# A fused Mamba and gated FFN layer in fp32: Silu of z read from PSUM, softplus as one function, dt products in row pairs, conv in place, the first norm on ScalarE, and new order lists

## The reference

```python
xz = jnp.einsum('bld,ed->ble', x, W_in)            # 256 -> 1024
xi, z = jnp.split(xz, 2, axis=-1)                  # 512 each
xc = sum((xpad[:, k:k + L, :] * conv_w[:, k] for k in range(4)))
u = silu(xc + conv_b)
dbl = jnp.einsum('blc,ec->ble', u, W_xproj)        # 512 -> 16 + 16 + 16
dt = jax.nn.softplus(jnp.einsum('blr,cr->blc', dbl[..., :16], W_dt) + b_dt)
# scan over the tokens, 16 states for each of the 512 channels:
h = h * exp(dt * A) + (dt * u) * B ;  y = sum over states of h * C
y = (y + u * D_skip) * silu(z)
x = layernorm(x + y @ W_out.T)
x = layernorm(x + (silu(x @ wg.T) * (x @ wu.T)) @ wd.T)   # 256 -> 768 -> 256
```

## Time and profile before

| | |
|---|---|
| median of 3 runs | 1802.77 us |
| span of the profiled execution | 1797.7 us (5.1 us below the median of the runs, which have what lies around it too) |
| PE busy | 1734.7 us, 96% |
| ACT busy | 1712.9 us, 95% |
| DVE busy | 1675.1 us, 93% |
| POOL busy | 1477.8 us, 82% |
| ACT table loads | 125 of 1283 ns |

### The profile page before, as it was taken

One profiled execution on the slowest core, in us unless ns is written; L12 is line 12 of the kernel. 1 busy time (PEld: TensorE's weight loads), 2 busy tenths in 40 slices (PEclk: granted clock), 3 DMA queues, 4 the chain that ended last, 5 costly groups with the idle time before them and its releaser, 6 DMA issues.

```text
span 1797.7 us, 40378 instructions
## 1 busy us (share of the span) xinstructions
PE 1734.7 (96%) x15678; PEld 1214.6 (68%) x15678; DVE 1675.1 (93%) x1970; ACT 1712.9 (95%) x2907; POOL 1477.8 (82%) x852
## 2 busy tenths in 40 slices
PE   7779999999999999999999999999999999999997
PEld 3456676767667676676767667676676767667676
DVE  5999999999999999999999999999999999999974
ACT  6999999999999999999999999999999999999971
POOL 5897987979889797997979889797987979889850
PEclk9999999999999999999999999999999999999999
DMA  7040211304013030211304013040311304022000
GB/s 211 1 121 1 56 65 15 118 11 121 3 16 118 15 118 2 66 68 16 118 10 123 2 15 119 14 119 1 74 60 16 118 13 121 1 39 83 1 25 24
DMA packets 171487, 100.57 MB, mean 56 GB/s; under 512 B 139408, under 2 KB 157584, under 8 KB 163232
## 3 DMA queue, kind: packets, MB, share of 16 engines
q1 hardware_dynamic: 171296, 97.98, 19.3%
HBM read 88.52 MB, written 9.44 MB: 54 GB/s over the span
## 4 chain that ended last, share of the span: by engine, by line
PE 48%; ACT 26%; DVE 11%; issue 9%; POOL 5%; SPq 0%; DMA 0%; ACTq 0%; POOLq 0%; DVEq 0%
PE ring L1162 17%; PE tp L1141 13%; ACT decay L706 8%; ACT hT L713 7%; PE yb L1155 7%; DVE h L917 6%; POOL drive L568 4%; PE ring L1254 3%; PE ring L1230 3%; DVE acc L938 3%; PE ring L1199 2%; ACT L743 1%; ACT acc L722 1%; PE ring L1220 1%; ACT dt L760 1%
## 5 line engine op out<-in xcount | busy, mean ns | idle before, releaser
L568 POOL TENSOR_TENSOR drive<-dtu,b_all 128x1024 f32<-128x1024 f32 x511 | 1204.4, 2389 | 17.6 <-DVE acc L938 9.2
L706 ACT ACTIVATE decay<-dt,a_neg 128x512 f32<-128x512 f32 x1024 | 705.0, 717 | 7.2 <-DVE h L917 6.4
L917 DVE TENSOR_TENSOR_SCAN h<-decay,h,drive 128x512 f32<-128x512 f32 x512 | 620.5, 1267 | 9.4 <-ACT decay L706 6.4
L1141 PEld LDWEIGHTS tp<-ident,h 128*128 128x128 f32 x4096 | 463.9, 141 | 240.1 <-issue 124.1
L917 DVE TENSOR_TENSOR_SCAN h<-decay,drive 128x512 f32<-128x512 f32 x512 | 592.3, 1208 | 29.2 <-ACT decay L706 25.3
L713 ACT ACTIVATE hT<-tp 128x512 f32<-128x512 f32 x1024 | 595.9, 618 | 11.8 <-PE tp L1141 10.9
L1141 PE MATMUL tp<-ident,h 128*128 128x128 f32 x4096 | 564.1, 277 | 37.9 <-ACT hT L713 29.1
L1155 PE MATMUL yb<-hT,diag_c 128*32 128x128 f32 x8192 | 275.8, 277 | 6.5 <-ACT yt L734 5.3
L1155 PEld LDWEIGHTS yb<-hT,diag_c 128*32 128x32 f32 x8192 | 210.7, 110 | 82.5 <-issue 48.8
L1162 PE MATMUL ring<-xt,w_in 128*128 128x512 f32 x512 | 245.2, 602 | 2.3 <-ACT acc L754 2.3
L1162 PE MATMUL ring<-xt,w_g 128*128 128x512 f32 x360 | 170.6, 596 | 0.0
(11 more groups left out here) (132 smaller groups left out, 1648.1 us busy)
## 6 DMA issues: line engine op xcount, KB each, us to landing
b_all<-bc_scratch SPq DMA_DIRECT2D x63, 1024.0 KB, 7.2
xt<-in_xT SPq DMA_DIRECT2D x16, 512.0 KB, 4.7
res<-in_x SPq DMA_DIRECT2D x16, 512.0 KB, 6.6
out<-res SPq DMA_DIRECT2D x15, 512.0 KB, 2.9
c_col<-bc_scratch SPq DMA_DIRECT2D x256, 2.0 KB, 2.4
bc_scratch<-dbl SPq DMA_DIRECT2D x16, 64.0 KB, 1.6
b_all<-bc_scratch SPq DMA_DIRECT2D x2, 512.0 KB, 4.4
w_g<-in_w_gT SPq DMA_DIRECT2D x1, 768.0 KB, 6.3
```

Source lines behind the costliest of these rows:

```text
L568: tt(drive[:, j % 4, :, :], src, b_all[:, n:n + 2, :], ALU.mult).then_inc(g_dr, 1)
L706: act(decay[decay_slot(k.parity, i)][:, :], dt[:, cb, :], ACT.Exp, scale=a_neg[:, cb, n:n + 1]).then_inc(a_da, 1)
L917: nc.vector.tensor_tensor_scan(h[:, h_slot(k.parity, q), at:at + T, i % 4], decay[decay_slot(k.parity, i)][:, :], drive[:, (i // 2) % 4, i ...
L1141: last = nc.tensor.transpose(tp[g % 2][:, b * P:(b + 1) * P], h[:, h_slot(k.parity, q), t0:t0 + TS, :].rearrange("p t s -> p (t s)"), iden ...
```

## The change

- `silu_z` reads z's PSUM bank itself; `copy_z` goes. The bank is free only when the Silu is done.
- Softplus is one activation function, read from the dt bank. The bias b_dt comes in as one more row of the product: `w_dt` has the row, and `dbl` has a 1 there (`one_at`, added while it is copied).
- `dbl` holds the two halves of the tokens on the partition halves 0 to 63 and 64 to 127, in 256 columns. `dt_pair` makes two blocks at a time with four products of 64 rows and 256 columns; the upper and the lower half of the rows go to different banks. `dt` now has two buffers, by parity of the chunk.
- The conv runs in place in `u`; `acc` goes.
- The first norm is applied by ACT; `normalise` has a parameter for it.
- `hT` has nine slots for eight. `out` and `down` are cut into halves that can be placed apart.
- The tables are new, and the first and last chunk use the steady ones (only POOL's first stays). The three output products that stood in the last chunk's table now stand in PE_END. SP stores `dbl` with two DMAs, and loads W_dt and b_dt twice.

```diff
-HTS = 8
+HTS = 9
-    (2, 2): [("hT", 4), ("xi", 0), ("z", 2), ("hT", 5)], (2, 3): [("hT", 6)], (3, 0): [("hT", 7)],
+    (6, 0): [("sz", 0), ("y", 0), ("sz", 1), ("norm", 0), ("u", 0), ("sz", 2), ("sz", 3), ("hT", 17), ("hT", 18), ("x1T", 0), ("x1T", 1), ("u", 1), ("hT", 19), ("hT", 20), ("u", 2), ("u", 3), ("tanh", 0)],
...
+PE_FIRST = PE_LAST = PE_SIDE
+ACT_FIRST = ACT_LAST = ACT_SIDE
+DVE_FIRST = DVE_LAST = DVE_SIDE
+POOL_LAST = POOL_SIDE
...
-                wait(eng, v_dt, k.count(2, -1 + cb // 2))
+                wait(eng, v_y, k.count(4, cb - 7))
...
-                act(acc[:, cb, :], bank(k, "xi", cb)[:, :], ACT.Identity, scale=cw[:, cb, KW - 1:KW],
+                act(u[:, k.parity, cb, :], bank(k, "xi", cb)[:, :], ACT.Identity, scale=cw[:, cb, KW - 1:KW],
...
             def silu_z(k, cb):
-                eng.wait_ge(a_z, k.count(4, cb + 1))
-                act(sz[:, cb, :], sz[:, cb, :], ACT.Silu).then_inc(a_sz, 1)
+                wait(eng, p_z, k.count(4, cb + 1))
+                wait(eng, g_y, k.count(4, cb - 3))
+                act(sz[:, cb, :], bank(k, "z", cb)[:, :], ACT.Silu).then_inc(a_sz, 1)
...
+                act(dbl[:, :], bank(k, "xproj", 0)[:, 0:T // 2], ACT.Identity, bias=one_at[:, 0:1]).then_inc(a_dbl, 1)
+
+            def softplus(k, p):
+                wait(eng, p_dt, k.count(4, 2 * p + 2))
+                wait(eng, g_dtu, k.count(2, p - 3))
                 for b in range(2):
+                    act(dt[:, k.parity, 2 * p:2 * p + 2, b * T // 2:(b + 1) * T // 2],
+                        bank(k, "dt", 2 * p + b)[:, :].rearrange("p (c t) -> p c t", c=2), ACT.Softplus).then_inc(a_dt, 1)
...
-            def softplus_max(k, half):
-                stt(dt[:, two, :], dt[:, two, :], 40.0, acc[:, two, :], ALU.min, ALU.max).then_inc(v_dt, 1)
...
+            def dt_pair(k, p):
+                wait(eng, a_dbl, k.count(1, 1))
+                for c in range(2):
+                    for b in range(2):
+                        rows = slice(b * RB, (b + 1) * RB)
+                        block = slice((2 * p + c) * P, (2 * p + c + 1) * P)
+                        last = mm(bank(k, "dt", 2 * p + b)[:, c * T // 2:(c + 1) * T // 2], w_dt[rows, block], dbl[rows, :],
+                                  start=True, stop=True)
+                        if c == 1:
+                            last.then_inc(p_dt, 1)
```

More of the change, by code:

```diff
@@ L31 @@
 KW = 4
+RB = 64
 HD = 768
@@ L51 @@
 PE_SIDE = {
[L52 to L62, removed]
+    (0, 1): [("xi", 0)], (0, 3): [("sum", 14), ("sum", 15)], (1, 0): [("turn", 3)], (1, 1): [("xi", 1)],
@@ L63 @@
+    (10, 2): [("up", 3)], (11, 0): [("dt", 1), ("sum", 8), ("sum", 9)],
+    (11, 2): [("turn", 1), ("gate", 4), ("gate", 5)], (12, 0): [("up", 4)], (12, 1): [("up", 5)],
+    (12, 3): [("sum", 10), ("sum", 11)], (13, 1): [("down", 0, 0), ("turn", 2)], (13, 3): [("down", 0, 1)],
+    (14, 1): [("sum", 12)], (14, 3): [("down", 1, 0), ("down", 1, 1)], (15, 3): [("sum", 13)],
 }
 ACT_SIDE = {
[18 rows of a table removed]
[16 rows of a table added]
 }
 DVE_SIDE = {
-    (2, 1): [("skip", 3)], (3, 3): [("conv", 0, 0), ("r1", 0)], (4, 2): [("r1", 1)],
-    (5, 3): [("max", 1), ("norm", 0), ("conv", 0, 1), ("conv", 1, 0), ("conv", 1, 1), ("conv", 2, 0), ("conv", 2, 1), ("conv", 3, 0), ("conv", 3, 1)],
@@ L106 @@
-ACT_FIRST = {
[16 rows of a table removed]
[L123 to L129, removed]
+    (2, 1): [("diag", 1), ("gate", 3)], (5, 0): [("diag", 2)], (5, 1): [("diag", 3)], (6, 0): [("std", 0)],
+    (6, 1): [("heads", 0)], (7, 0): [("dtu", 1)], (12, 0): [("dtu", 0)], (12, 1): [("std", 1)],
@@ L267, in in_chunk @@
 def in_chunk(item, kind):
-    what, i = item
+    what, i, *part = item
     if what in TAIL or item == ("turn", CB - 1):
@@ L272, in in_chunk, with banks_of @@
     return what not in HEAD or kind != "last"
+def banks_of(item):
+    what, i, *part = item
+    if what == "dt":
+        return [(what, 2 * i), (what, 2 * i + 1)]
+    if what == "sum" or what.startswith("end_") or part and part[0] > 0:
+        return []
+    return [(what, i)]
 def owner(what, i, c):
@@ L288, in products_in_order @@
 def products_in_order(chunks):
-    before = [item for at in sorted(PE_FIRST) for item in PE_FIRST[at] if item[0] in HEAD]
-    order = [(what, i, 0) for what, i in before]
+    order = [(what, i, 0) for item in PROLOGUE for what, i in banks_of(item)]
     for c in range(chunks):
@@ L294, in products_in_order @@
         table = table_of(kind, PE_SIDE, PE_FIRST, PE_LAST)
-        order += [(what, i, owner(what, i, c)) for at in sorted(table) for what, i, *_ in table[at]
-                  if what != "sum" and not what.startswith("end_") and in_chunk((what, i), kind)]
+        order += [(what, i, owner(what, i, c)) for at in sorted(table) for item in table[at]
+                  if in_chunk(item, kind) for what, i in banks_of(item)]
     return order
@@ L622, in item @@
                     scale_and_shift(k + (-2 if i else -1), i)
-                if what == "std" and i == 0 and not head:
-                    eng.wait_ge(v_x1, (k + -1).count(4, 4))
                 if what == "first_diag":
@@ L630, in item @@
                     diagonals(k, i)
-                if what == "yield" and head:
-                    wait(eng, v_conv, conv_steps(k + 1, 1))
                 if what == "heads" and head:
@@ L810, in item @@
                         copy_y(k + -1, i)
-                if what == "norm" and late:
-                    normalise(k + -2)
+                if what == "norm" and i == 1 and late:
+                    normalise(k + -2, 1)
+                if what == "norm" and i == 0 and tail:
+                    normalise(k + -1, 0)
                 if what == "x1T" and tail:
@@ L1025, in _ @@
             for cb in range(CB - 1):
-                conv(k0, cb, 0)
-                conv(k0, cb, 1)
+                for step in range(KW - 1):
+                    conv(k0, cb, step)
             eng.wait_ge(l_w, ALL_LOADED)
@@ L1246, in gate_up, with down, dense @@
                                    for d in range(DH)], done)
-            def down(k, i):
-                if i == 0:
+            def down(k, i, half):
+                if i == 0 and half == 0:
                     wait(eng, v_hid, k.count(6, 6))
-                for half in range(2):
-                    tb = 2 * i + half
-                    for m in range(HB):
-                        last = mm(bank(k, "down", i)[:, half * DM:(half + 1) * DM],
-                                  hidden_block(m)[:, tb * P:(tb + 1) * P],
-                                  w_d[:, m, :], start=m == 0, stop=m == HB - 1)
-                last.then_inc(p_down, 1)
-            def dense(k, what, i):
+                tb = 2 * i + half
+                for m in range(HB):
+                    last = mm(bank(k, "down", i)[:, half * DM:(half + 1) * DM], hidden_block(m)[:, tb * P:(tb + 1) * P],
+                              w_d[:, m, :], start=m == 0, stop=m == HB - 1)
+                if half == 1:
+                    last.then_inc(p_down, 1)
+            def dense(k, what, i, *part):
                 if what == "xi":
@@ L1290, in item @@
                 elif in_chunk((what, *of), kind):
-                    c = owner(what, *of, k.index)
-                    room(place[what, *of, c])
+                    c = owner(what, of[0], k.index)
+                    for name, i in banks_of((what, *of)):
+                        room(place[name, i, c])
                     dense(k + (c - k.index), what, *of)
@@ L1397, in _ @@
             eng.wait_ge(l_in[0], 16)
-            for at, (what, i, c) in enumerate(order):
-                if c > 0 or what not in HEAD:
-                    break
+            for what, i in PROLOGUE:
                 if (what, i) == ("xi", 1):
@@ L1410, in _ @@
                     eng.wait_ge(l_w, ALL_LOADED)
-                room(at)
+                for name, n in banks_of((what, i)):
+                    room(place[name, n, 0])
                 if what == "xproj":
```

256 lines of the change are left out of this document (89 added, 167 removed), and 63 rows, old and new, of tables (ACT_FIRST, ACT_LAST, ACT_SIDE).

## The result

The changed kernel takes 2083.67 us (median of 4 runs, 2083.41 to 2088.32), the kernel before 1802.77 beside it. The ratio is 1.157, with an interval of 1.1549 to 1.159. Now and then an execution of a kernel falls into a much slower state (one of the four before took 2961.67 us); medians and ratios here leave such executions out. The forecast was 1755 us with a range to 1788: wrong in sign, and by 329 us.

The account below looks back on a forecast made before the run. PE and ACT were both taken as full. Savings of 40.6 us (14 steady chunks), 5 (chunk 0) and 2 (last chunk), with 0.5 added (head), gave span 1750.6, plus 5.1 about 1755; own range 1742 to 1768, 8-in-10 range 1734 to 1788.

Parts of the forecast that it names:

- the one on SP: SP's store of dbl becomes two; it need only finish before the next chunk's drives, with 15 us POOL idle: 0.
- row pairs: PE's dt products: eight of 64 rows and 256 columns share the array, 1.72 us saved a chunk; shape changes add 0.25.
- Rival 2: PE's dt row pairs do not share the array: +1.72 us on 15 chunks, 1781 us; chance 0.12.
- PE's idle time: PE in steady chunks: half of its idle 1.05 us goes, since ACT is no longer full.
- the 104.9 of the forecast: Steady chunk: 107.8 us less 2.4 of PE work and half of PE's idle 1.05, so 2.9 saved.
- rival 3: PE waits on its two product banks (z on Silu, gate on DVE): 1.6 us a chunk, 1777 us; chance 0.18.
- the block without a decay: ACT between the switches to and from the Silu table: about 13 us without decays, DVE's cover lacking about 1.
- Rival 4: Slower: ACT's 13 us block and DVE's conv steps don't overlap, DVE lacks decays: 4.8 us a chunk, 1822; chance 0.08.
- the drain: ACT table loads: the skill page's 1.38 us per load, 8.3 us for six, left out because the trace disagrees.
- Chunk 0: First chunk: between POOL's 94.9 us busy and the 104.1 it took; 99 taken, 5 saved.
- Tail: The 54.8 us behind the last chunk's last scan: same work, change 0.
- The output products: PE, last chunk: those moved behind the last scan cost there what they save here; the chunk saves 2 us.

Follow-up runs that it names:

- run 1: Changed kernel with SP's store of out moved behind all other DMA issues of the chunk; 1798.76 us, ratio 0.9994 to the kernel before.
- run 5: As run 1, with heads in POOL's list of chunk 0 moved from (8, 0) to (6, 1); 1793.42 us, ratio 0.9963 to the kernel before.
- run 3: Kernel before, with only ACT's second norm moved from (6, 3) to (14, 3); 2089.07 us, ratio 1.1605.
- run 6: As run 1, with ACT's second norm moved from (14, 3) to (13, 3); 1819.12 us, ratio 1.0103 to the kernel before.
- run 12: As run 5, with the first norm back on DVE ahead of the conv steps; 1797.88 us, ratio 0.9984 to the kernel before.
- Runs 7 and 10: Last chunk's lists changed, down and output products earlier: 7 on run 1, 1804.07 us; 10 on run 5, smaller, PE's list alone, 1795.03 us.
- run 8: Kernel before, with SP's store of out moved behind all other issues of the chunk; 1800.16 us, ratio 0.9999.
- run 9: As run 5, with turn 3 behind xi 1, tanh 1 and 2 behind evacuations 23 and 25, evacuations 55 and 56 earlier; 1891.85 us, ratio 1.051.
- run 11: As run 5, with the four products of a dt pair issued by row half, not in turn; 1793.85 us, ratio 0.9968 to the kernel before.

## Why the prediction was wrong

From its span of 1750.6 to the measured 2081.6 it is 331 us. Run 1 takes back 281.3 of that (2081.6 - 1800.3), run 5 another 8.7 (to 1791.6), and 41 remain.

**The step that failed** is the one on SP: "SP only has to be done before the next chunk's drives, which have 15 us of POOL idle behind them: 0". It counted the added DMA and not what stands ahead of it. The second norm's move from (6, 3) to (14, 3) has no term in the sum at all; with its work on ACT unchanged, it was put at nothing without a reason. But the store of `out` waits for it, at the head of a queue that everything for the next chunk has to pass. The row was there to be read: in the kernel before SP already waited 66 us a chunk for that norm.

```profile
SPq L488 <- ACT res L772: 132.1, 2, 66.4
```

The norm now came 49 us later, with 23 DMAs behind the store that the next chunk needs, and the chunk grew by 20.6 to 21.3 us; run 3 shows that this move alone does it (1.1605), run 1 that the queue carries it. No rival had this mechanism; the slower one was put on ACT's block against the conv steps.

**PE, row pairs: right.** The pair shares the array, 0.86 us and 0.20 for changes of shape. Rival 2 is refuted. In run 5 PE's busy time is 105.1 on average against 106.8, 1.7 saved and not 2.4; where the other 0.7 went was not traced.

**PE's idle time: wrong in sign.** Half of 1.05 was to go, "since ACT is no longer full". It grew to 1.5 (105.35 - 104.25 = 1.1 and 107.85 - 105.96 = 1.9). Together with the 0.7 above, this 1.0 is the 1.7 us by which a steady chunk of run 5 misses the 104.9 of the forecast. In run 5 PE waits for evacuations 2.5 us in two chunks where it was 1.3, though ACT idles 5 to 6 us a chunk:

```profile
PE tp L1030 <- ACT hT L648: 2.5, 7, 0.9
```

I read this as PE waiting for the place of an evacuation in ACT's list, and not for ACT's load: moving ACT's norm (run 6) or taking one off it (run 12, with more for DVE) freed nothing. No run shows it by itself. This is rival 3 in kind, though on the transpose banks, and small: 106.5 a chunk and not 104.9, 21 us over 13 chunks.

**ACT: right.** Six table loads a chunk and softplus as in the first rows below (two steady chunks of run 1), the block without a decay 12.75 us in run 5 (13 forecast), behind which DVE waited 0.9 (1 forecast). Rival 4 didn't come: DVE waited 2.6 us for decays in two chunks. On the drain that the Trainium skill (page "ScalarE: Activation LUTs", section "What ACT_TABLE_LOAD costs") adds to a load: there is none in these rows either. The last two rows are from run 5, and the decay starts as the load of 1.28 us ends.

```profile
L641 ACT ACT_TABLE_LOAD x6 | 7.7, 1283 | 0.1
...
L688 ACT ACT_TABLE_LOAD x4 | 5.1, 1283 | 0.1
...
L688 ACT ACTIVATE dt<-ring 128x512 f32<-128x512 f32 x8 | 4.4, 597 | 0.0
L673 ACT ACT_TABLE_LOAD x2 | 2.6, 1283 | 0.0
```

```profile
928.14 1.28 ACT L641 ACT_TABLE_LOAD   x1
929.43 1.91 ACT L641 ACTIVATE decay<-dt,a_neg 128x512 f32<-128x512 f32 x3
```

**Chunks 0 and 1.** Chunk 0 was forecast at 99 and is 103.5 even in run 5. PE idles 26 us in it, but it idled 28 in the kernel before too, so this does not say why the 5 us did not come; only the place of heads was tested. Chunk 1 takes 111.0 and not 104.9. It starts on a PE at half the clock: 50 matmul records in its first 5.6 us, 77 in those of chunk 3. Yet the clock is not the main cause: in the changed kernel chunk 1 had a granted clock of 1.00 and took 110.3, as the row below shows. What holds it was not traced.

```profile
139.67:250.01 110.34, 107.12 (x1004) 76.56 (x1006) 101.89 (x117) 100.44 (x175) 96.13 (x51) 1.00 0.18 50
```

**Tail: wrong.** "Same work, 0" was measured as +6.6 (61.4 against 54.8). The output products that "cost there what they save here" saved next to nothing in the last chunk, 101.2 against 101.7: PE's work there fell by 5.5 us (99.6 to 94.1) and its idle time grew by nearly as much. Runs 7 and 10 suggest that they are in the tail's sum, but not how to get them out.

The 41 us are then: 13 steady chunks 21, chunk 1 6, tail 6.6, chunk 0 4.5, last chunk 1.5, head 1.4.

## What to carry to other kernels

When an instruction moves in one engine's list, follow its result into every queue, and ask what stands *behind* the instruction that waits for it; a DMA queue whose issues leave in program order, as SP's did here, turns a late result nobody needs into a late load everybody needs. Put such stores last: here that costs nothing when the result is early (run 8) and saves 285 us when it is late (run 1). And where two buffers are used in turn, the order of uses is part of the program: run 9, with one swapped pair, lost 98 us, and its trace puts the 3.9 us wait of each chunk on that pair.

## What the runs showed of the hardware

- Row halves of the array ran side by side in both orders of the program: with neighbours on the same rows (run 11) the eight records took the same 1.14 us, and they start in four pairs as before. So products of one half seem to have started ahead of earlier ones of the other; the records do not name the half, so this is inferred.
- A first conv step on DVE took 7.9 us (0.73 in steady chunks) while POOL ran back to back beside it, and ended 0.5 us after POOL's last instruction; with POOL stopped there it was gone (run 5). The conv step reads xi and u, both in SBUF. The scans, which take decay from PSUM and only drive from SBUF, were not held beside the same POOL work. The Trainium skill, page "SBUF — State Buffer", section "SBUF: two separate sides", has a rule that fits: DVE with two SBUF inputs and a GpSimd instruction that reads SBUF share a port pair as an exclusive lock, for a whole instruction each. That the lock is the cause no run here shows apart. If it is, the run adds that the loser can wait through three whole instructions in a row.
- The granted clock had been 1.00 from chunk 1 to chunk 14 of the kernel before. Waits of PE of 12 us in each chunk of the changed kernel, and of 3.9 us in run 9, were followed by products at half that clock (0.53 and 0.50). In run 9 the four products behind the wait took 1.9 us more than at 1.00, so this stall of PE cost more than its length; the chunk lost 7.4 us in all, with two other moves in it.
